# Attention stream: value matmuls and output turns moved, mask clearing left out, probability turns issued ahead of the scores

## What is computed

```python
x = x + tanh(g_xattn[1]) * _L1_xattn_ref(_layernorm(x), ctx_2048, mask, wq, bq, wk, bk, wv, bv, wo, bo)
x = x + tanh(g_ffn[1]) * _L1_ffn_ref(_layernorm(x), W1, W2)
...
q = _w8a8_linear(x, wq, bq)          # rows rounded to 127 levels, 16 heads of 32
k = cond @ wk.T + bk; v = cond @ wv.T + bv
scores = einsum('bhnd,bhld->bhnl', q, k) * inv_sqrt_d + mask
attn = softmax(scores)
o = einsum('bhnl,bhld->bhnd', attn, v)
return _w8a8_linear(o, wo, bo)       # rows of o rounded again
...
h = silu(_bitlinear(x, W1)); return _bitlinear(h, W2)
```

## Time and profile before

| | us |
|---|---|
| median of three runs | 1121.09 |
| lowest and highest run | 1118.70, 1126.54 |
| the profiled execution's own time | 1122.45 |
| its span, first to last instruction | 1120.7 |

### The profile page before, as it was taken

How to read it: one execution, slowest core, us unless ns; L and a number is a source line. 1 busy time by engine, 2 the same in 40 slices (tenths; PEclk the granted TensorE clock), 3 DMA queues, 4 the chain that set the end, 5 groups by cost and what they waited for, 6 DMA issues and landing times.

```text
span 1120.7 us, 16359 instructions
## 1 busy us (share of the span) xinstructions
PE 949.5 (85%) x5904; PEld 630.0 (56%) x5912; DVE 736.1 (66%) x1945; ACT 574.9 (51%) x1124; POOL 133.2 (12%) x121
## 2 busy tenths in 40 slices
PE   3999799999999869898788887898878888798567
PEld 2777576777677557676555554354544555445223
DVE  5888852625341356877577888758877678677554
ACT  3444231212221347776577777656775666856252
POOL 4444100000000001112010020010200102001200
PEclk9999899999999989999899998999989999899769
DMA  6330400202011276687986533046330550002000
GB/s 210 112 113 35 151 1 1 76 1 75 1 41 73 76 294 249 255 309 237 308 193 139 140 86 85 1 130 153 86 85 1 160 123 1 1 1 76 1 1 38
DMA packets 60928, 115.37 MB, mean 103 GB/s; under 512 B 7088, under 2 KB 15280, under 8 KB 59824
## 3 DMA queue, kind: packets, MB, share of 16 engines
q1 hardware_dynamic: 52048, 88.62, 27.5%
q0 software_dynamic: 6016, 25.17, 5.8%
q10 hardware_dynamic: 2784, 0.54, 0.2%
HBM read 84.95 MB, written 29.36 MB: 102 GB/s over the span
## 4 chain that ended last, share of the span: by engine, by line
PE 34%; issue 11%; DVE 9%; ACT 8%; DMA 2%; POOL 1%; SPq 0%; DVEq 0%; POOLq 0%; ACTq 0%
PE psum L1501 7%; PE psum L1591 5%; PE psum L1569 5%; PE psum L1517 4%; PE psum L1492 4%; DVE probsT L1809 2%; PE psum L1364 2%; ACT hqT L1319 1%; PE psum L1366 1%; PE psum L1365 1%; DVE neg_max L1800 1%; ACT probs L1291 1%; PE psum L1556 1%; PE psum L1428 1%; DVE o_rows L1826 1%
## 5 line engine op out<-in xcount | busy, mean ns | idle before, releaser
L1800 DVE CUSTOM_DVE_ANT_0 psum<-psum,m_in 128x512 f32<-128x512 f32 x256 | 176.9, 696 | 59.9 <-issue 53.4
L1291 ACT ACTIVATE probs<-psum,neg_max 128x512 f32<-128x512 f32 x256 | 176.2, 690 | 71.1 <-DVE neg_max L1800 68.1
L1501 PE MATMUL psum<-ident,probs 128*128 128x128 f32 x1024 | 161.1, 282 | 42.5 <-DVE o_rows L1826 34.1
L1501 PEld LDWEIGHTS psum<-ident,probs 128*128 128x128 f32 x1024 | 126.5, 145 | 76.5 <-ACT probs L1291 38.9
L1492 PE MATMUL psum<-k,q 128*128 128x512 f32 x256 | 130.3, 511 | 7.5 <-DMA k<-k_dram 6.2
L505 PE MATMUL psum<-w_sb,hT 128*128 128x512 f32 x256 | 115.1, 593 | 0.0
L1283 ACT COPY probsT<-psum 128x512 f32<-128x512 f32 x128 | 74.6, 583 | 53.0 <-PE psum L1501 52.7
L389 ACT ACTIVATE hT<-psum,b_col 128x256 f32<-128x256 f32 x64 | 26.8, 469 | 136.4 <-PE psum L425 136.4
L1809 DVE COPY probsT<-psum 128x512 f32<-128x512 f32 x128 | 87.9, 687 | 4.6 <-PE psum L1501 4.0
L423 PE MATMUL psum<-xselT_hi,w_hi 128*128 128x256 f32 x256 | 82.8, 323 | 4.2 <-ACT onehotT L383 4.2
L1517 PE MATMUL psum<-probsT,vv 128*32 128x256 f32 x1024 | 85.4, 409 | 0.0
(11 more groups left out here) (227 smaller groups left out, 1800.1 us busy)
## 6 DMA issues: line engine op xcount, KB each, us to landing
q<-q_dram SPq DMA_DIRECT2D x64, 256.0 KB, 8.0
k<-k_dram SPq DMA_DIRECT2D x64, 256.0 KB, 5.3
c_in<-in_ctx_dram SPq DMA_DIRECT2D x8, 1024.0 KB, 5.0
bw_in<-in_L_ffn_W_dram SPq DMA_DIRECT2D x8, 1024.0 KB, 8.4
xres<-in_x_dram SPq DMA_DIRECT2D x4, 1024.0 KB, 5.1
w_raw<-in_L_ffn_w_dram POOLq DMA_DIRECT2D x4, 1024.0 KB, 5.1
w_sb<-in_L_ffn_w_dram SPq DMA_DIRECT2D x1, 4096.0 KB, 13.6
x_mid_dram<-xres SPq DMA_DIRECT2D x4, 1024.0 KB, 4.5
```

Source lines behind the costliest of these rows:

```text
L1291: act.activation(probs[:, s % 4, :], psum[s % SCORE_BANKS][:, :], ACT.Exp, scale=-1.0, bias=neg_max[:, s % UNITS:s % UNITS + 1], accum_out ...
L1501: mm = pe.transpose(turn_bank(n)[:, l * P:(l + 1) * P], probs[:, u % 4, l * P:(l + 1) * P], ident[:, :])
L1800: dve.tensor_tensor_reduce(bank[:, :], bank[:, :], m_in[:, nt, :], -1.0, LOWEST, ALU.add, ALU.min, neg_max[:, s % UNITS:s % UNITS + 1]).th ...
```

## The change

- `AV_STEPS` becomes (0, 2, 4, 6): value matmuls at places 3, 5, 7 and 1. `AV_COPY`, `O_TURN` and `O_SCALE` become 18, 20 and 21: places 2, 4 and 5. `SIDE_FIRST` follows and is 14, not 12, so each piece of side work comes two steps later. `unit_turn` and `o_turn` number the turns accordingly.
- ScalarE copies the even units and VectorE the odd ones: VectorE's copies fall on even places.
- The clearing of `held` is left out of the stream, 256 instructions of VectorE.
- On TensorE the turn of unit s - 3 stands ahead of the scores of unit s.
- Batch 0 of the projections: `k_hi` and `k_lo` of blocks 0 and 1 come ahead of the normalisation of the queries and of their scales.
- SyncE issues the first two groups of k loads when the chunk of `bw_in` under each has been turned (`bwT_psum` 10 and 12).
- For the last batch VectorE, not GpSimd, rounds the attention rows and the rows before the feed-forward block (eight instructions), new functions `rounded_attention` and `rounded_rows` on VectorE.

```diff
-        AV_STEPS = (1, 2, 4, 5)
-        AV_COPY, O_TURN, O_SCALE = AV_FIRST + 6, AV_FIRST + 7, AV_FIRST + 8
+        AV_STEPS = (0, 2, 4, 6)
+        AV_COPY, O_TURN, O_SCALE = AV_FIRST + 7, AV_FIRST + 9, AV_FIRST + 10
...
-            return u + max(0, u // UH - 1)
+            return u + max(0, (u - O_TURN + LAG + UH - 1) // UH)
...
-            return min(UH * (n + 2), NU) + n
+            return min(UH * n + O_TURN - LAG + 1, NU) + n
...
                     biased_rows(b)
-                    rounded_attention(b)
+                    if b + 1 < B:
+                        rounded_attention(b)
                     residual_rows(b)
-                    rounded_rows(b)
+                    if b + 1 < B:
+                        rounded_rows(b)
...
+                for g in range(2):
+                    sp.wait_ge(bwT_psum, 8 + 2 * g + 2)
+                    load_keys(0, g)
                 sp.wait_ge(bwT_psum, 16)
-                load_keys(0, 0)
-                load_keys(0, 1)
...
                     key_highs(b, range(1))
+                    if b == 0:
+                        key_highs(b, range(1, 2))
+                        normed_queries(b)
...
-                    if 0 <= u < NU and u % 2 == 1:
+                    if 0 <= u < NU and u % 2 == 0:
...
-                normed_queries(0)
...
                 def attend(s):
+                    u = s - LAG
+                    if 0 <= u < NU:
+                        n = unit_turn(u)
+                        pe.wait_ge(probs_ready, u + 1)
+                        if n >= 2:
+                            turn_wait(pe, n - 2)
+                        for l in range(T):
+                            mm = pe.transpose(turn_bank(n)[:, l * P:(l + 1) * P], probs[:, u % 4, l * P:(l + 1) * P], ident[:, :])
+                        mm.then_inc(turn_psum, 1)
                     if s < NU:
...
-                    u = s - LAG
-                    if 0 <= u < NU:
...
+                    if b == 0:
+                        key_low(b, 0)
+                        key_low(b, 1)
                     query_scales(link, b)
...
                         dve.wait_ge(score_psum, s + 1)
-                        dve.memset(held[:, s % 4:s % 4 + 1], 0.0)
...
-                    if 0 <= u < NU and u % 2 == 0:
+                    if 0 <= u < NU and u % 2 == 1:
...
+                def rounded_attention(b):
+                    dve.wait_ge(o_inv_ready, b + 1)
+                    for t in range(T):
+                        dve.tensor_scalar(xn[:, t, :], o_rows[:, t, :], o_inv[:, t:t + 1], TURN, ALU.mult,
+                                          ALU.add).then_inc(oq_ready, 1)
```

More of the change, by code:

```diff
@@ L1233, in project @@
                     rounded_queries(b)
-                    key_highs(b, range(1, 2))
+                    if b:
+                        key_highs(b, range(1, 2))
                     if b == 2:
@@ L1755, in project @@
                     more = b + 1 < B
+                    if b == 0:
+                        key_low(b, 0)
+                        key_low(b, 1)
                     query_scales(link, b)
-                    key_low(b, 0)
+                    if b:
+                        key_low(b, 0)
                     if b % 2:
@@ L1761, in project @@
                         turned_bw(0, (0, 2))
-                    key_low(b, 1)
+                    if b:
+                        key_low(b, 1)
                     if b == 2:
@@ L1842, in attention_scales, with rounded_rows @@
                     link(dve.tensor_scalar(o_gain[:, :], o_scale[:, :], gate_x1, None, ALU.mult))
+                def rounded_attention(b):
[3 more added lines that the diff above has]
+                                          ALU.add).then_inc(oq_ready, 1)
+                def rounded_rows(b):
+                    dve.wait_ge(inv_ready, b + 1)
+                    for t in range(T):
+                        dve.tensor_scalar(xn[:, t, :], xn[:, t, :], inv[:, t:t + 1], TURN, ALU.mult,
+                                          ALU.add).then_inc(xq_ready, 1)
                 def scaled_out(b, t):
@@ L1925, in side @@
                         attention_scales(b, link)
+                        if b + 1 == B:
+                            rounded_attention(b)
                     if 10 <= j < 10 + T:
```

## The result

| | before | after |
|---|---|---|
| median of four timed runs (lowest to highest) | 1123.18 us (1118.7 to 1126.54) | 1154.87 us (1144.06 to 1158.13) |
| profiled execution | 1122.45 us | 1158.13 us |
| its span | 1120.7 us | 1156.4 us |
| granted clock over the span | 0.955 | 0.955 |

The ratio after to before is 1.0268, interval 1.0189 to 1.0346: slower by 31.7 us between the medians. Between the two profiled executions it is 35.7 us. The forecast was 1169 with a range of 1138 to 1198: the sign and the range hold, the size is 14 us too large by the medians.

The account below looks back on a forecast made before the run. No engine was full (TensorE busy 85%); a plain half-group's other 2.1 us were waits for turn banks, most for the output turn's scaling. 1122.45 + 56 - 2 - 5.3 - 1.7 = 1169.5, stated as 1169, range 1138 to 1198.

Parts of the forecast that it names:

- Turns ahead of the scores: Order on TensorE in the stream: the deciding term, summed over the 32 half-groups to +56 us.
- the chain: Turns that VectorE copies: turn, scores, mask instruction, copy, release; 2.51 us until the next turn may use that bank.
- the walk: Once round a half-group, waits at places 6-0, 0-2, 2-4, 4-5, 5-6: sum 12.84 us against 10.8 measured, +2.05.
- the twelve plain half-groups: Half-groups without side work, six of batch 0, two each of the others: 12 x 2.05 = +25 us.
- first two of batch 0: First two half-groups of batch 0: four chains of 2.51, 10.0 us against 8.0; +2 each, +4.
- second: Second half-groups of batches 1 to 3: 14.2 us against 10.9, VectorE's pieces half hidden; +3.3 each, +10.
- fourth: Fourth half-groups, VectorE full with scaling and statistics: about 16.5 us against 14.3; +2.3 each, +7.
- turn to the scores behind it 0.55: First link on TensorE, from the turn's start to the scores' weight load: 0.55 us, read at 606.34 to 606.89.
- The first k loads: Loads before the first scores: issued at 525.1, landing long before 540.7, ending TensorE's 6.20 us wait; -5.3 us.
- The clock: Rival: TensorE's clock falls in most half-groups, 1.1 us left for about 24 of 32, total 1195; chance 0.13.
- Faster: Rival: VectorE's chain under 2.11 us, so the 2.1 us of waits go instead; total 1085; chance 0.12.
- No change: Rival: side half-groups hide all, only plain ones and first two pay 29; 1130 or just under; chance 0.09.

Follow-up runs that it names:

- the two kernels by parity: Changed kernel with the turn ahead of the scores only at odd places: 1109.53 us; only at even places: 1125.02 us.
- the kernel with the order alone: Kernel before with only the turn put ahead of the scores of its step: 1188.73 us, ratio 1.0578.
- the fullest kernel, the quarter moved: Changed kernel with scores ahead of the turn again and the first quarter of value matmuls at place 4: 1092.60 us, ratio 0.9716.
- the chain opened: Changed kernel with the scores ahead of the turn again, all else kept: 1102.43 us, ratio 0.9819.
- starts and tail alone: Kernel before with only the new order of batch 0's projections, early k loads and last roundings on VectorE: 1118.81 us, ratio 0.9974.

## Why the prediction was right, and what it mis-sized

**Turns ahead of the scores (+56 forecast, about +40 in the trace).** The mechanism was right. Taking the order back gives 50 us, opening the chain at another link (the copy ahead of the mask instruction) gives 34 without touching the order, and each wait that the walk names was there with its place. By terms, forecast and trace (from mask instruction to mask instruction, 39.7 in all): the twelve plain half-groups +25 and +15.2; first two of batch 0 +4 and +3.6; first of batches 1 to 3 +3 and -0.1; second +10 and +8.5; third +3 and +3.3; fourth +7 and +5.9; fifth 0 and -0.4; the one with the feed-forward block +4 and +3.6.

The step that was mis-sized is the first link of the chain, "turn to the scores behind it 0.55". It was read at 606.34 to 606.89, from a turn that ran directly behind running scores. In the chain the turn has just waited, and the link is 0.38 or 0.39 (606.78 to 607.16, 609.12 to 609.51). The state makes the difference, not the kernel: in the changed kernel too a turn directly behind scores takes 0.54 (611.72 to 612.26), and the trace of before had a turn that had waited, in the half-group that the prediction read, at 0.39:

```profile
601.72 0.42 PEld L1501 LDWEIGHTS psum<-ident,probs 128*128 128x128 f32 x4 [0.38 <-issue]
...
602.11 0.19 PEld L1492 LDWEIGHTS psum<-k,q 128*128 128x128 f32 x1
```

Five links of 0.165 us too much are 0.83, and 12.84 - 0.83 is 12.0, what was measured. Twelve times 0.83 is 10 us, most of the miss. The other links stood: 0.55, 0.61, 0.69 and 0.11 for 0.54, 0.61, 0.69 and 0.12.

Some of the other terms came near by luck. The fourth half-group was forecast at 12.84 + 3.6, about 16.5, and measured at 16.2 to 16.3; with the link put right the same sum gives 15.6. All three of them had a stretch at half clock (a clock of 0.89 to 0.90 over the half-group), and where the kernel with the clearing put back had none, such a half-group took 15.3 for 16.3. So a link that was too long stood in for a fall of the clock that the forecast left out. The second, forecast at 14.2, took 14.0 twice with such a fall and 13.3 without one, where the corrected sum gives 13.4. The first two of batch 0, four chains, would be 9.4 with the right link and took 9.9: here too something was left out, and no run says what.

That the plain half-group came out right after this correction doesn't prove each step of the walk by itself, but two were tried alone: the quarter of value matmuls (0.5 us, forecast 0.57), and the parity. There the prediction's account was complete: it had the scaling in its walk (2.23 for the step from 5 to 6, 2.08 measured). My later expectations for the two kernels by parity weren't: I forgot that this place is odd.

**The first k loads (-5.3 forecast, about -3.8).** "Issued there, they land long before 540.7" failed. The first four were issued from 527.7 on, and the slowest of them landed 16.6 us after its issue, for 7.4 before. The stretches of the changed kernel there show the DMA engines full (the last but one number is their share):

```profile
530.00:540.00 10.00, 9.60 (x69) 7.93 (x70) 7.32 (x9) 2.12 (x2) 3.66 (x2) 0.83 1.04 410
540.00:547.00 7.00, 4.13 (x22) 2.83 (x19) 3.03 (x5) 2.40 (x2) 0.75 (x1) 1.00 1.04 371
```

Most of the earlier issue was spent behind other loads. Moving four q loads behind the first k loads ended the wait, which is what one expects if the bytes ahead of them, and not the moment of issue, set when they land.

**The smaller terms.** The projections gave 1.4 us where 2 were forecast, the roundings' part of the kernel 2.7 where 1.7 were (in the kernel with these edits alone 3.0; this part varies by about 1 us from trace to trace), the clearing 0 as forecast.

**The rivals.** *The clock* did fall more often in the changed kernel, though the mean over the span, 0.955 as before, hides it: in 11 of the 32 half-groups for 7, for 44 us of the stream at half clock for 35. It isn't the fall in most half-groups that the rival needs: ten of the twelve plain ones stayed at 1.00. Two plain ones side by side show what a fall cost here, 1.3 us:

```profile
758.70:770.70 12.00, 9.05 (x76) 5.44 (x75) 8.37 (x23) 8.84 (x23) 3.06 (x3) 1.00 0.86 249
770.70:784.00 13.30, 10.56 (x77) 6.68 (x76) 8.41 (x23) 8.82 (x23) 1.94 (x2) 0.87 0.66 155
```

With 9 us more at half clock, in which half the work is done, the rival explains a few of the 40 us at most. In the kernel with the order alone the clock fell in 25 half-groups. There the waits of TensorE stand close together; in the changed kernel value matmuls and turns lie between them. That this is the reason is argued, not shown. The Trainium skill's rule on transposes ("TensorE: Matmul & The Clock Gate", Part 4) would have it fall in most half-groups. The trace didn't bear that out: some 34 of the 76 to 81 matmuls of a plain half-group are transposes, and it stayed at 1.00 in ten of twelve here, and in the stretch of 9.20 us of the fullest kernel. What transposes count for beside other matmuls no run here can tell.

*Faster* was to be decided at a chain of 2.1 us; with 2.34 it wasn't reached, but with the chain opened the time was 1102, and 1093 with the quarter moved, near its 1085. So its premise (the rest of the change fits better) was right. Beside 1118.81 for starts and tail alone, 1102.43 puts some 17 us of gain (0.9974 to 0.9819) on the new places and the other parity, which no run took apart (the clearing, in the same step, gives nothing).

*No change* (whose own terms add up to 1131, not just under 1130) fell with the side half-groups, which hid only a part. In sum, by the ratios: +50 for the order, -17 for places and parity, -3 for starts and tail make the +30 us of 1.0268.

## What to carry to other kernels

- When one instruction is moved ahead of another on one engine, follow the resource that it takes round the whole loop, through the program order of the engine that gives it back. Here two instructions swapped on TensorE closed a loop that ran through VectorE's unchanged program, and cost 4.6%.
- Take the price of a link from an instance in the same state as in the loop: one that has just waited, not one that runs behind other work. Here both stood in one half-group of the trace before, 0.39 and 0.55; the range between them belongs in the forecast.
- A change of several edits can be slower while most of them help. Undoing or moving one at a time gave the kernel at 0.969 of before, out of one at 1.027.

## What the runs showed of the hardware

- From the start of the first weight load of four f32 transposes (128x128) to the start of the weight load behind them: 0.38 or 0.39 us after a wait, 0.54 or 0.55 directly behind scores.
- The mean busy share of a half-group doesn't tell whether its clock falls. One of 12.0 us with TensorE busy for 9.02 stayed at 1.00; one of 13.7 us with TensorE busy for 10.63 had a stretch with 1.26 us of work in 3.41, and a stretch at 0.50 behind it. Such a fall cost 1.3 us in a plain half-group of the changed kernel and 1.4 in the kernel with the order alone.
- The mean clock of a span hides where it fell: 0.955 before and after, with 7 and with 11 half-groups in which it did.
- Four k loads took 3.8 to 7.4 us to land before, and 10.6 to 16.6 us when they were issued 14 us earlier in the stage, at a share of the DMA engines of 1.0 in both kernels. The wait for them became shorter by only 3.5 us.
- A VectorE instruction of 59 ns in front of one of 696 cost nothing that the runs could tell, in a kernel with VectorE 70% busy in the half-group and in one with 90%.
